# One fused layer, an output projection's bias added once, the result stored in four tiles, and fewer idle products

## The reference

```
x = x + xattn(ln(x), ctx, ctx)      # 8 batches of 64 queries, 1601 context rows, 16 heads of 16
                                    # xattn: out @ Wo.T + bo
x = x + causal_attn(ln(x))          # 64 tokens of a batch, no biases
x = x + moe(ln(x))                  # 8 experts: 256 -> 1024 (exact gelu) -> 256, top 2 of a softmax
```

## Time and profile before

| what | value |
|---|---|
| median of 3 runs | 684.64 us (683.98 to 685.73) |
| the profiled execution | 684.26 us, its span 682.4 us |
| TensorE busy | 655.0 us, 96% of the span |
| VectorE busy | 473.3 us, 69% |
| ScalarE busy | 326.9 us, 48% |
| GpSimd busy | 296.1 us, 43% |

### The profile page before, as it was taken

The page is one execution under the profiler, slowest core; times in us unless marked ns, Lnnn a source line. Parts: engine busy times, 40 slices in busy tenths (PEclk is TensorE's granted clock), DMA queues, the critical chain, the costliest instruction groups (busy, mean ns, idle before and its releaser), DMA issues.

```text
span 682.4 us, 16188 instructions
## 1 busy us (share of the span) xinstructions
PE 655.0 (96%) x6618; PEld 538.7 (79%) x6626; DVE 473.3 (69%) x870; ACT 326.9 (48%) x533; POOL 296.1 (43%) x386
## 2 busy tenths in 40 slices
PE   7989999999999989999999999979999999999996
PEld 4778878878867867877887787656788999999996
DVE  4887757667657688584977857479778666666653
ACT  4355655554454554455446453446555444444431
POOL 1137797896676688675668766400000000000000
PEclk9999999999999999999999999999999999999999
DMA  5311110100010010011001000062003203320000
GB/s 164 144 49 51 28 48 26 49 26 26 26 35 16 26 50 25 26 34 41 9 20 48 1 2 1 2 248 88 37 1 124 103 22 124 123 109 14 0 0 31
DMA packets 12853, 34.12 MB, mean 50 GB/s; under 512 B 1515, under 2 KB 9972, under 8 KB 10612
## 3 DMA queue, kind: packets, MB, share of 16 engines
q1 hardware_dynamic: 12756, 33.19, 14.6%
q0 software_dynamic: 32, 0.01, 0.0%
HBM read 32.67 MB, written 0.52 MB: 49 GB/s over the span
## 4 chain that ended last, share of the span: by engine, by line
PE 81%; DVE 9%; issue 5%; ACT 2%; POOL 2%; DMA 0%; POOLq 0%; DVEq 0%; ACTq 0%
PE bank L1154 45%; PE bank L1340 13%; PE bank L1163 9%; PE bank L1224 5%; POOL prob_sum L481 2%; PE bank L1264 2%; PE bank L1273 2%; DVE prob_sum L481 1%; DVE ctx_lo L465 1%; DVE maxes L877 1%; ACT probs L719 1%; ACT k_hi L615 1%; PE bank L1248 1%; DVE k_lo L858 1%; PE bank L1370 1%
## 5 line engine op out<-in xcount | busy, mean ns | idle before, releaser
L481 POOL TENSOR_TENSOR prob_sum<-probs,prob_sum 128x256 f32<-128x256 f32 x336 | 266.3, 824 | 80.6 <-ACT probs L719 76.3
L719 ACT ACTIVATE probs<-bank 128x1024 f32<-128x1024 f32 (+1 forms) x104 | 106.6, 1025 | 122.9 <-PE bank L1340 107.9
L877 DVE TENSOR_REDUCE maxes<-bank 128x1 f32<-128x400 f32 (+1 forms) x256 | 131.3, 566 | 21.6 <-PE bank L1224 19.7
L701 ACT ACTIVATE h_raw<-bank,b_sb 128x512 f32<-128x512 f32 (+2 forms) x72 | 46.1, 641 | 106.5 <-PE bank L1154 106.3
L858 DVE SCALAR_TENSOR_TENSOR k_lo<-bank,bias_sb,k_hi 128x400 fp32r<-128x400 f32 (+2 forms) x64 | 40.4, 632 | 50.3 <-ACT k_hi L615 50.2
L1154 PE MATMUL bank<-w_hi,h_hi 128*128 128x256 f32 x256 | 72.7, 284 | 0.0
L1154 PE MATMUL bank<-w_hi,h_lo 128*128 128x256 f32 x256 | 72.2, 282 | 0.0
L1340 PE MATMUL bank<-qbd_hi,k_hi 64*128 64x256 f32 (+1 forms) x416 | 71.8, 339 | 0.3 <-issue 0.3
L1154 PE MATMUL bank<-w_lo,h_hi 128*128 128x256 f32 x256 | 72.1, 281 | 0.0
L1163 PE MATMUL bank<-probs,v_sb 128*32 128x128 f32 (+1 forms) x1664 | 67.0, 279 | 2.5 <-DVE masked L812 2.0
L1154 PE MATMUL bank<-wv_hi,ctx_hi 128*128 128x256 f32 (+1 forms) x208 | 65.2, 314 | 2.2 <-DVE maxes L877 1.9
(11 more groups left out here) (157 smaller groups left out, 1427.0 us busy)
## 6 DMA issues: line engine op xcount, KB each, us to landing
raw<-in_w SPq DMA_DIRECT2D x16, 1024.0 KB, 6.8
ctx_raw<-in_ctx_t SPq DMA_DIRECT2D x16, 400.0 KB, 3.7
ctx_raw<-in_ctx_t SPq DMA_DIRECT2D x8, 402.0 KB, 3.6
ctx_raw<-in_ctx_t SPq DMA_DIRECT2D x8, 399.0 KB, 3.6
w_sb<-in_w_t SPq DMA_DIRECT2D x1, 1280.0 KB
w_raw<-in_w_t SPq DMA_DIRECT2D x2, 256.0 KB, 4.6
result<-x_all SPq DMA_DIRECT2D x1, 512.0 KB, 3.0
x_all<-in_x SPq DMA_DIRECT2D x1, 384.0 KB, 4.2
```

Of the source, the lines that this page charges most:

```text
L481: ins = engine.tensor_tensor(prob_sum[0:ROWS[k], cols], probs[0:ROWS[k], s % 2, cols], acc[0:ROWS[k]], ALU.add)
L701: nc.scalar.activation(h_raw[:, c % 2, 0:width], bank[:, at, 0:width], ACT.Gelu, bias=b1_sb[:, bass.ds(e, 1), c:c + 1].rearrange("p a b -> ...
L719: nc.scalar.activation(probs[0:ROWS[k], s % 2, :].rearrange("p (g n) -> p g n", g=G), bank[0:ROWS[k], score_bank(b, k):score_bank(b, k) + ...
L877: nc.vector.tensor_reduce(maxes[:, g * PAIRS + j, c:c + 1], src[:, 0:width], AX.X, ALU.max).then_inc(read_dve, 1)
```

## The change

There are three independent parts.

1. `WARM_UP` goes from (6, 12) to (6, 8): four idle products fewer, just ahead of K0.
2. The product of the bias row leaves all four y1 units. In its place there is one new unit, "bias", in step 13 of the first tile (`REST_CHAIN`): TensorE makes the 128 x 256 product of ones and `bo_all` once, and VectorE adds it, repeated four times, to all of `x_all` (128 x 1024). VectorE waits there for the unit and for all four normalisations of the input (`xn_ready`), and in front of each y1 add for the count of reads that tells that this add is done.
3. At the end, TensorE's last `output` counts each bank (`y_bank`) as its two tiles are complete; VectorE runs four gated sums, two behind each count, and SyncE stores a tile (128 KB) as its sum is done, with four transfers in place of one of 512 KB.

```diff
-WARM_UP = (6, 12)
+WARM_UP = (6, 8)
-REST_CHAIN = {3: ["p1"], 5: ["r1"], 6: ["p2"], 8: ["r2"], 9: ["p3"], 11: ["r3"]}
+REST_CHAIN = {3: ["p1"], 5: ["r1"], 6: ["p2"], 8: ["r2"], 9: ["p3"], 11: ["r3"], 13: ["bias"]}
...
-            sp.wait_ge(y_taken, E)
-            sp.dma_start(out, x_all[:, :, :]).then_inc(stored, 16)
-            sp.wait_ge(stored, 16)
+            for t in range(TT):
+
+                sp.wait_ge(y_taken, E + t)
+                sp.dma_start(out[:, t:t + 1, :], x_all[:, t:t + 1, :]).then_inc(stored, 16)
+            sp.wait_ge(stored, 16 * TT)
...
+                elif kind == "bias":
+
+                    dve.wait_ge(xn_ready, TT)
+                    nc.vector.tensor_tensor(x_all[:, :, :], x_all[:, :, :],
+                                            src[:, 0:D].unsqueeze(1).broadcast_to([P, TT, D]), ALU.add)\
+                        .then_inc(read_dve, 1)
                 elif kind in ("y1", "y2"):
 
+                    if kind == "y1":
+                        dve.wait_ge(read_dve, bias_added)
...
-            dve.wait_ge(y_chunk, chunk_of_all(E, 0))
-            gated_sum(E - 1, 0, TT, 6)
+            for t in range(TT):
+                dve.wait_ge(y_bank, t // 2 + 1)
+                gated_sum(E - 1, t, t + 1, 6)
...
                     for g in range(G):
-                        nc.tensor.matmul(dst[:, 0:D], o_t[:, g, :], w_sb[:, 1, g, :], start=(g == 0), stop=False)
-                    ins = nc.tensor.matmul(dst[:, 0:D], ones_f[0:1, :], bo_all[:, :], start=False, stop=True)
+                        ins = nc.tensor.matmul(dst[:, 0:D], o_t[:, g, :], w_sb[:, 1, g, :], start=(g == 0),
+                                               stop=(g == G - 1))
+                elif kind == "bias":
+
+                    ins = nc.tensor.matmul(dst[:, 0:D], ones_f[0:1, :], bo_all[:, :], start=True, stop=True)
...
+                    if by_bank and t % 2:
+                        ins.then_inc(y_bank, 1)
+                if not by_bank:
+                    ins.then_inc(y_chunk, 1)
```

More of the change, by code:

```diff
@@ L446, in perceiver_kernel @@
         y_taken = sem("y_taken")
+        y_bank = sem("y_bank")
         stored = sem("stored")
@@ L607, in unit @@
                     return
-                if kind == "M" or kind in ("y1", "s0", "s1", "o0", "o1", "y2", "b2"):
+                if kind in ("M", "bias", "y1", "s0", "s1", "o0", "o1", "y2", "b2"):
                     return
@@ L848, in queries_lo @@
                         op1=ALU.subtract).then_inc(q_split if g < G - 1 else done, 1)
+            bias_added = FIRST.before[2] + FIRST.counts(1 + next(n for s in range(STEPS) for n, kind, _ in FIRST.at[s]
+                                                                 if kind == "bias"))[2]
             def unit(units, n, kind, u, t, b, parity):
@@ L1427, in hidden, with output @@
                                for d in range(DC)]).then_inc(h_psum, 1)
-            def output(i, c, n, at, first, last):
+            def output(i, c, n, at, first, last, by_bank=False):
                 pe.wait_ge(h_split, n + 1)
@@ L1439, in output @@
                                         start=(c == 0 and (t % 2 == 0 or t == first)), stop=(c == HC - 1), skip_group_check=True)
-                ins.then_inc(y_chunk, 1)
+                    if by_bank and t % 2:
+                        ins.then_inc(y_bank, 1)
+                if not by_bank:
+                    ins.then_inc(y_chunk, 1)
             def alone(s):
@@ L1507, in _ @@
             for c in (HC - 2, HC - 1):
-                output(1, c, chunk_of_all(E - 1, c), 6, 0, TT)
+                output(1, c, chunk_of_all(E - 1, c), 6, 0, TT, c == HC - 1)
 def kernel(**a):
```

## The result

| kernel | runs | median us | lowest to highest |
|---|---|---|---|
| before, beside the changed one (its first three are the three runs of the table of times before) | 20 | 686.30 | 682.99 to 688.84 |
| changed | 20 | 683.68 | 680.69 to 685.09 |

The ratio of the changed kernel to the one before is 0.9956, with a 95% interval of 0.9938 to 0.9973. It is faster by 0.44%, some 3.0 us. Forecast were 680.5 us and 0.6%; the direction held, but 683.68 lies outside the range of 679.2 to 682.6. Of the miss of 3.18 us, 1.66 is the level: the kernel before now stands at 686.30, and the forecast started from 684.64. The forecast gain of 4.15 us still lies inside the interval, which is 1.9 to 4.3 us.

A forecast was written before the change was run, and what follows sets the result against it. TensorE was taken as the bound, simply full from 36 to 478 us. The terms -0.85 - 2.45 - 0.15 + 0.7 - 1.4 = -4.15 us, on a median of 684.64, gave 680.5 us, range 679.2 to 682.6.

The forecast's parts named there:

- the four places: The opening, step 13 of the first tile, the four y1 units and the last 8 us, where the change acts.
- TensorE is simply full: Between 36 and 478 us: TensorE's longest wait entry is 3.1 us in two pieces, in a stretch of 442 us.
- rival C: Opening: with fewer idle products TensorE's clock rises late or falls back, up to 9 us more, 689.5 us; chance 0.03.
- Opening, -0.85: Ahead of K0: four idle products go and the clock rises at the same moment, 0.85 us gained; bounds 0.2 to 1.7.
- the low bound's case: Opening: the clock rises much earlier and K0 is held by the K weights' low part; only some 0.2 us gained.
- y1, -2.45: Tiles 1 to 3: removing the bias product from three y1 units saves 0.82 us each; low bound 1.9 in all.
- Tail, -0.15: Fourth y1 unit: VectorE is busy with h_lo, so x1 comes at most 0.15 us earlier; bounds 0 and 0.8.
- Bias, +0.7: Step 13, first tile: the bias product costs TensorE 0.7 us (0.6 to 0.8); VectorE's add is hidden in its idle time.
- End, -1.4: Last sums and store: last store issued 0.6 us earlier and landing 0.8 us faster; bounds 1.1 to 1.5.
- Rival B: End: the split store brings nothing, or only 0.3 us from the sums; about 681.7 us, chance 0.12.

The follow-up runs named there:

- the filled kernels: Kernel before, changed kernel and single-part versions, each with 23 idle products in TensorE's waits in the last tile's second half; kernel before so filled: 683.91 us.
- f_after: The changed kernel with 23 idle products in TensorE's waits in the last tile's second half; 680.10 us, ratio 0.9927 to the kernel before.
- f_store: The kernel before with the 23 idle products in the last tile and only the bank-by-bank sums and four stores; 682.57 us, ratio 0.9971.
- after_again: The changed kernel measured once more, unaltered, beside the single-part kernels; 682.87 us, ratio 0.9951 to the kernel before.
- the second comparison: The changed kernel measured once more, in 8 runs, against 30 runs of the kernel before; means 683.07 and 686.44 us, ratio 0.9951.
- warm_only: The kernel before with only WARM_UP (6, 8), no gaps filled; 686.84 us, ratio 0.9986; executions keeping the clock 682.99 us.
- f_bias: The kernel before with the 23 idle products in the last tile and only the bias added once instead of in y1; 682.02 us, ratio 0.9952.
- bias_only: The kernel before with only the bias added once instead of in y1, no gaps filled; 685.26 us, ratio 0.9972.
- store_only: The kernel before with only the bank-by-bank sums and four stores, no gaps filled; 685.01 us, ratio 0.9975.
- after_late: The changed kernel with 12 idle products added in the first tile's bias unit, moving the gaps back in time; 684.13 us, ratio 0.9975.

## Why the prediction was wrong, point by point

- **What bounds the kernel: the step that failed.** TensorE, as read; the four places behaved as told. But of the waits only the longest entry was read, 3.1 us in two pieces, and "TensorE is simply full" put the loss of clock behind a wait at nothing; rival C had it at 0.03, for the opening alone. The two longest single waits stand right under that entry in the same view:

```profile
PE bank L1306 <- DVE gate_tile L930: 2.7, 1, 2.7
PE bank L1163 <- DVE masked L812: 2.0, 1, 2.0
```

  The runs showed in its place that around these waits the clock falls in 53 of 96 executions of the kernel before and in 27 of 28 of the changed one. Over all executions of the first comparison that is 2.1 us of mean loss before (686.29 against 684.2) and 3.0 after (683.24 against 680.2).
- **Opening, -0.85.** It shifted by 0.89 in the profiled execution and by 0.77 in the medians of the filled kernels. The moment of the rise is not fixed, as I had assumed it. In the changed kernel the eight idle products took 3.62 us (above), in f_after 1.89:

```profile
5.27 1.89 PE L1397 MATMUL bank<-ones_bf 128*128 128x512 bf16 x8
...
8.60 0.45 PE L1170 MATMUL bank<-ctx_hi,wk_hi 128*128 128x402 f32 x1 [1.44 <-DVE wk_lo L1002]
```

  There the clock was up before them, and K0 waited 1.44 us for `wk_lo`. That is the low bound's case; the term is an average over executions. The thirteen traces with idle products bear it out: with twelve idle products K2 starts between 14.65 and 15.43 us (seven traces, 15.13 on average), with eight between 13.91 and 14.51 (six traces, 14.19), so 0.9 for the part, with 0.6 to 0.8 of spread within either. The rule of the Trainium skill that I cited (TensorE: Matmul & The Clock Gate (Part 1)), that the number of products at the low level changes from run to run, agrees with this.
- **y1, -2.45.** -0.83, -0.82 and -0.63, together -2.28. The third is smaller since in tile 3 no V product follows y1, but `weigh`. Before, from the first `o_t` product to the next unit it was 385.26 - 383.69 = 1.57 us; after, 382.77 - 381.81 = 0.96; so 0.61. I had read one tile for three. Timelines, before and after:

```profile
383.69 1.03 PE L1232 MATMUL bank<-w_sb,o_t 128*128 128x256 f32 x4
384.64 0.69 PE L1233 MATMUL bank<-bo_all,ones_f 1*128 1x256 f32 x2
385.26 0.65 PE L1163 MATMUL bank<-probs,v_sb 128*32 128x128 f32 x16
```

```profile
381.81 1.03 PE L1247 MATMUL bank<-w_sb,o_t 128*128 128x256 f32 x4
382.77 0.65 PE L1178 MATMUL bank<-probs,v_sb 128*32 128x128 f32 x16
```

- **Tail, -0.15.** -0.28. TensorE's wait for `xn` grew from 0.15 to 0.69, as told (0.7).
- **Bias, +0.7.** +0.68. VectorE's add fitted into its hole.
- **End, -1.4.** -1.34 in the medians of the filled kernels, -1.2 in the trace. The two halves of it were each off, to opposite sides, so that the sum comes this near is in part luck. The last store is issued at 679.4, which is 1.8 us after the start of the last product (677.58); before it was 678.99 - 676.98 = 2.01. That is 0.2 earlier, not 0.6: the four issues take 2.11 us together in place of the 4 x 0.39 = 1.56 that the sums' distance would give. The landing fell by 1.0 (3.0 to 2.0), not 0.8. Rival B is out. The rule to coalesce many small transfers into one (DMA: Bandwidth & Descriptors of the Trainium skill, Rules for kernel authors) speaks against four stores; f_store's 1.34 us at a held clock do not agree with it at this place, where only the last 128 KB are waited for. The rows of the four (duration in ns least/median/most, first and last start; then the time to landing, least/median/most):

```profile
L535 SPq DMA_DIRECT2D result<-x_all x4: 342/390/447, 677.7 to 679.4; - x4
...
DMA to landing us min/median/max: 1.7/2.0/2.1
```

- **Rival C** had the right mechanism at the wrong place. I priced it in the opening, where idle products were removed, and gave it 0.03. It came 430 us later, where nothing was edited.
- **The level.** 684.64 was the median of three runs, all between 683.98 and 685.73. Of 96 later executions of the kernel before with their clock on record, 43 keep it, at 684.2; the rest take 685.7 to 691.8. The trace that I read was a keeping execution (granted clock 1.00), and I took its level for the kernel's time.

Summed up: 684.2 - 3.97 = 680.2 is what the changed kernel takes when the clock is held (its keeping execution in after_again: 680.72). Its median is 683.68, so some 3.4 us are the clock. The kernel before loses too, 2.1 from 684.2 to 686.3, but less. So of the 3.97 us, 3.97 - (3.4 - 2.1) = 2.7 are left between the medians (686.30 - 683.68 = 2.6). By the means it is 3.05 (686.29 and 683.24), and 3.4 in the second comparison, both with some 1 to 2 us of uncertainty either way: that the changed kernel loses more to the clock than the kernel before is likely by the medians and not shown by the means. That both lose some 2 to 3 us, which the forecast had at nothing, is shown.

**What stays open.** Which of the gaps, 1.99 or 2.67, matters more was not tried by filling one at a time; two traces show only that the second is enough. Why a shift by 1.6 us turns the odds and one by 0.8 hardly does, I did not find; the runs show only that it does. The early and the late place were not run side by side on one chip. Only the profiled execution of a kernel shows where its clock fell; for the others there is the mean. In the profiled execution of warm_only, the slowest of all (span 689.5, mean clock 0.983), it also fell once in the experts' part, from 516.3 to 526.5 us, with no wait of TensorE over 0.7 us in the 48 us before; no experiment was made on that, and it means that a full stretch is no guarantee. Seven executions of the filled kernels (six of the table and one of f_bias) still lost some clock and weren't looked into.

## What to carry to other kernels

Look for the places where TensorE waits for 2 us or so in an otherwise full stretch, and treat each as a place where the clock can fall: a change anywhere ahead of it that moves it in time can change how often it does. Fill them with idle products before comparing two versions, or compare only executions with the same granted clock; otherwise a part worth 0.8 to 1.2 us reads as nothing (warm_only). Count the time lost too, and not only how many executions lost some: bias_only had none that kept the clock and still brought its 1.9 us in the mean. Before forecasting an absolute time, ask whether the few runs at hand show all the levels that the kernel has. A price read in one tile counts for another only if the same unit follows there.

## What the hardware showed

- A wait of 1.99 us and one of 2.67 us, the same in every trace without the filling, go with a mean granted clock under 0.998 in some executions and not in others: in 53 of 96 of the kernel before, in 27 of 28 of the changed one.
- 23 idle products of 512 columns in these waits and in one of 1.05 us bring the kernel before from 685.87 to 683.91 us, no more than its executions at a held clock take (684.15).
- The clock can fall without such a wait too: it did in six of 48 executions of the filled kernels, whose longest wait left is 1.6 us (for `shift`), and at 516.3 us in the trace of warm_only.
- In two executions (after_again, bias_only) the clock fell while TensorE still waited, at 455.1 and 455.0 us in the wait of 2.67 us; in four others (changed, store_only, warm_only, after_late) it fell 0.9 to 1.6 us after the end of either wait.
- A store of 512 KB lands in 3.0 us, four of 128 KB in flight together in 2.0 each.
- SyncE's four issues start between 677.7 and 679.4, 0.57 us apart on average, though the four sums that release them take 1.66 us together, some 0.4 each.
